# Linear attention and experts on one core: sums kept in PSUM, denominators on VectorE, one-piece half swap, another order on TensorE

## What is computed

```python
q = q * cos + _rotate_half(q) * sin
k = k * cos + _rotate_half(k) * sin
qf = jax.nn.elu(q) + 1.0
kf = jax.nn.elu(k) + 1.0
def step(carry, inp):
    state, z = carry
    q_s, k_s, v_s = inp
    state = state + k_s[..., :, None] * v_s[..., None, :]
    z = z + k_s
    num = jnp.einsum('bhe,bhed->bhd', q_s, state)
    den = jnp.einsum('bhe,bhe->bh', q_s, z)[..., None] + EPS
    return ((state, z), num / den)
```

## Time and profile before

| | us |
|---|---|
| median of 3 runs | 1166.92 (1160.2 to 1170.29) |
| the profiled execution | 1166.46 |
| its span, first to last instruction | 1164.7 |
| PE busy | 954.9 (82%) |
| DVE busy | 801.9 (69%) |
| ACT busy | 497.5 (43%) |
| POOL busy | 662.7 (57%) |

### The profile page before, as it was taken

The page is one execution under the profiler, slowest core; times in us unless marked ns, Lnnn a source line. Parts: engine busy times, 40 slices in busy tenths (PEclk is TensorE's granted clock), DMA queues, the critical chain, the costliest instruction groups (busy, mean ns, idle before and its releaser), DMA issues. The chain is left out here.

```text
span 1164.7 us, 14438 instructions
## 1 busy us (share of the span) xinstructions
PE 954.9 (82%) x4439; PEld 772.0 (66%) x4439; DVE 801.9 (69%) x1561; ACT 497.5 (43%) x818; POOL 662.7 (57%) x568
## 2 busy tenths in 40 slices
PE   5889999999999999898579999998319668687881
PEld 3677777877777787776368888887318556565661
DVE  7877777777777778787265888888736565655650
ACT  5444454544454544455241211120206555656550
POOL 2778777777877777787300333334352555556552
PEclk9899999999999999999789999998559899888995
DMA  7011111101111111117143334412154887877842
GB/s 259 6 45 47 47 40 41 50 32 41 50 37 50 42 42 41 42 37 239 68 154 139 127 137 139 144 71 111 52 204 142 246 250 227 239 227 210 265 77 37
DMA packets 51654, 129.65 MB, mean 111 GB/s; under 512 B 11144, under 2 KB 13704, under 8 KB 45424
## 3 DMA queue, kind: packets, MB, share of 16 engines
q1 hardware_dynamic: 40144, 114.52, 28.3%
q0 software_dynamic: 11424, 14.07, 7.1%
HBM read 105.53 MB, written 35.72 MB: 121 GB/s over the span
## 5 line engine op out<-in xcount | busy, mean ns | idle before, releaser
L585 POOL TENSOR_TENSOR a_t<-a_t 128x512 f32<-128x512 f32 x80 | 122.6, 1533 | 52.0 <-DVE a_t L361 52.0
L1076 DVE TENSOR_TENSOR w_l<-raw,w_h 128x1024 fp32r<-128x1024 f32 x96 | 114.3, 1221 | 52.4 <-ACT w_h L1069 46.9
L1169 POOL DMA_INDIRECT out<-m_y,si x38 | 69.2, 1822 | 115.4 <-issue 55.2
L616 POOL TENSOR_TENSOR a_A_l<-a_A,a_A_h 128x512 fp32r<-128x512 f32 x64 | 84.7, 1324 | 60.6 <-ACT a_A_h L474 60.6
L216 PE MATMUL a_PQ<-w_h,a_xT_h 128*128 128x512 f32 x384 | 113.8, 422 | 4.0 <-DVE w_l L347 3.3
L1069 ACT ACTIVATE w_h<-raw 128x1024 fp32r<-128x1024 f32 x96 | 97.8, 1061 | 39.5 <-PE m_PY L1233 39.4
L782 PE MATMUL r_PY<-w_h,r_o_h 128*128 128x512 f32 x256 | 102.9, 402 | 9.9 <-DVE r_o_l L864 9.9
L216 PE MATMUL a_PQ<-w_l,a_xT_h 128*128 128x512 f32 x384 | 104.7, 395 | 0.0
L216 PE MATMUL a_PQ<-w_h,a_xT_l 128*128 128x512 f32 x384 | 103.9, 393 | 0.0
L782 PE MATMUL r_PY<-w_l,r_o_h 128*128 128x512 f32 x256 | 101.9, 398 | 0.0
L782 PE MATMUL r_PY<-w_h,r_o_l 128*128 128x512 f32 x256 | 101.7, 397 | 0.0
(11 more groups left out here) (186 smaller groups left out, 2478.5 us busy)
## 6 DMA issues: line engine op xcount, KB each, us to landing
raw<-in_wgu SPq DMA_DIRECT2D x32, 1024.0 KB
oT<-a_o SPq DMA_DIRECT2D x64, 256.0 KB, 2.5
raw<-in_wd SPq DMA_DIRECT2D x32, 512.0 KB, 5.9
v_l<-oT SPq DMA_DIRECT2D x11, 1024.0 KB, 5.6
v_h<-oT SPq DMA_DIRECT2D x5, 1024.0 KB, 5.4
out<-r_x SPq DMA_DIRECT2D x18, 256.0 KB, 2.0
a_xin<-in_x SPq DMA_DIRECT2D x16, 256.0 KB, 3.2
v_l<-in_wq SPq DMA_DIRECT2D x4, 1024.0 KB, 13.5
```

Source lines behind the costliest of these rows:

```text
L585: eng.tensor_tensor(t1[:, r % 2, :], t1[:, r % 2, :], t2[:, r % 2, :], ALU.add).then_inc(sm["xr"], 1)
L616: eng.tensor_tensor(A_l[:, n % 2, :], A[:, n % 2, :], f(A_h[:, n % 2, :]), ALU.subtract).then_inc(sm["Al"], 1)
L1076: eng.tensor_tensor(low, src, high.bitcast(F32), ALU.subtract).then_inc(sm["m_wl"], 1)
L1169: eng.indirect_dma_start(out[:, :], bass.IndirectOffsetOnAxis(ap=si[:, i:i + 1], axis=0), y[:, e % 2, t, :], None, compute_op=ALU.add).the ...
```

## The change

- `turned` now also transposes x; the bank PX is given up. Key sums have a bank of their own, PZ, and the state one, PU. `sum_k` adds the lower part of the chunk's sums onto what the bank holds, and `rest_k`, after `z_copy`, adds the other part, so that each row then holds the sum over all tokens so far. `update` adds to PU from chunk to chunk; S, `state`, z_h and z_l are gone, and S_h and S_l are made from PU (S_l on VectorE).
- `times_z` is gone. `reduce` makes four `tensor_tensor_reduce` over 128 columns each, which multiply, sum and add 1e-6.
- `rotate` makes t2 with one instruction of 128x512 that reads the halves swapped.
- The projections of a chunk come in the order K, Q0, Q1, V, Q2, Q3. On TensorE `score` stands right behind the projections, then transposes, then `attend` and `update`. VectorE begins an iteration with `reduce` and `feature_q` of earlier groups. K_h, K_l and z have two buffers for one, QT_h and QT_l three for two, V_h and V_l two for three.
- Eight weight pieces are split ahead of the loop, and four in each of the first iterations. Wo is loaded an iteration later.

```diff
         def unit_v(c):
-            return 6 * c + 1
+            return 6 * c + 3
 
         def unit_q(n):
-            return 6 * (n // 4) + 2 + n % 4
+            return 6 * (n // 4) + (1, 2, 4, 5)[n % 4]
...
-                    if c >= 1:
-                        eng.wait_ge(sm["S"], c)
-                    eng.matmul(PM[:, :], tri_r[:, :], K_h[:, :], start=True, stop=False)
-                    last = eng.matmul(PM[:, :], tri_r[:, :], K_l[:, :], start=False, stop=c == 0)
-                    if c > 0:
-                        eng.matmul(PM[:, :], last_r[:, :], z_h[:, :], start=False, stop=False)
-                        last = eng.matmul(PM[:, :], last_r[:, :], z_l[:, :], start=False, stop=True)
-                    last.then_inc(sm["zc"], 1)
+                    eng.matmul(PZ[:, :], tri_r[:, :], K_h[:, c % 2, :], start=c == 0, stop=False, skip_group_check=True)
+                    eng.matmul(PZ[:, :], tri_r[:, :], K_l[:, c % 2, :], start=False, stop=True,
+                               skip_group_check=True).then_inc(sm["zc"], 1)
+
+                def rest_k(c):
+
+                    eng.wait_ge(sm["z"], c + 1)
+                    eng.matmul(PZ[:, :], rest_r[:, :], K_h[:, c % 2, :], start=False, stop=False, skip_group_check=True)
+                    eng.matmul(PZ[:, :], rest_r[:, :], K_l[:, c % 2, :], start=False, stop=True, skip_group_check=True)
 
...
                 def update(c):
-                    eng.wait_ge(sm["zl"], c + 1)
-                    eng.wait_ge(sm["z"], c + 1)
+
+                    eng.wait_ge(sm["pqfree"], unit_v(c) + 1)
+                    if c >= 1:
+                        eng.wait_ge(sm["Sl"], c)
                     for g in range(4):
                         cols = slice(g * P, (g + 1) * P)
                         steps = [(K_h, V_h), (K_h, V_l), (K_l, V_h)]
                         for s, (a, b) in enumerate(steps):
-                            last = eng.matmul(PM[:, cols], a[:, cols], b[:, c % 3, cols],
-                                              start=s == 0, stop=s == 2)
+                            last = eng.matmul(PU[:, cols], a[:, c % 2, cols], b[:, c % 2, cols],
+                                              start=c == 0 and g == 0 and s == 0, stop=s == 2, skip_group_check=True)
                     last.then_inc(sm["u"], 1)
 
                 turn_x(0)
                 for n in range(NG + 5):
                     c, g = divmod(n, 4)
                     if g == 0 and c < NC:
-                        project(unit_k(c), c, 0)
-                        project(unit_v(c), c, 1)
+                        project(unit_k(c))
+                    if g == 2 and c < NC:
+                        project(unit_v(c))
                     if n < NG:
-                        project(unit_q(n), c, 2 + g)
-                    if 0 <= n - 5 < NG:
-                        attend(n - 5)
-                    if g == 0 and 1 <= c < NC:
-                        update(c - 1)
+                        project(unit_q(n))
+                    if 0 <= n - 4 < NG:
+                        score(n - 4)
                     if g == 1 and c < NC:
                         eng.wait_ge(sm["f"], rot_k(c) + 1)
-                        turned(fK[:, :], turn_k(c))
+                        turned(fK[:, :], turns["k", c])
                         sum_k(c)
                     if 0 <= n - 3 < NG:
                         eng.wait_ge(sm["fs"], n - 2)
-                        turned(fQ[:, (n - 3) % 3, :], turn_q(n - 3))
+                        turned(fQ[:, (n - 3) % 3, :], turns["q", n - 3])
+                    if 0 <= n - 5 < NG:
+                        attend(n - 5)
+                    if g == 1 and 1 <= c < NC:
+                        update(c - 1)
                     if g == 2 and c + 1 < NC:
                         turn_x(c + 1)
-                    if 0 <= n - 4 < NG:
-                        score(n - 4)
+                    if g == 3 and c + 1 < NC:
+                        rest_k(c)
...
                     if r >= 2:
                         eng.wait_ge(sm["f"], r - 1)
                     q = heads(PQ[u % 2][:, :])
-                    a, b = heads(t1[:, r % 2, :]), heads(t2[:, r % 2, :])
-                    sn = tab[:, c % 2, 1, :]
-                    eng.tensor_tensor(a, q, spread(tab[:, c % 2, 0, :]), ALU.mult)
-                    eng.tensor_tensor(b[:, :, 0:64], q[:, :, 64:128], spread(sn[:, 0:64]), ALU.mult)
-                    eng.tensor_tensor(b[:, :, 64:128], q[:, :, 0:64], spread(sn[:, 64:128]), ALU.mult).then_inc(sm["pqfree"], 1)
+                    swapped = q.rearrange("p h (s d) -> p h s d", s=2)[:, :, ::-1, :]
+                    sn = tab[:, c % 2, 1, :].rearrange("p (s d) -> p s d", s=2).unsqueeze(1).broadcast_to([P, 4, 2, 64])
+                    eng.tensor_tensor(heads(t1[:, r % 2, :]), q, spread(tab[:, c % 2, 0, :]), ALU.mult)
+                    eng.tensor_tensor(heads(t2[:, r % 2, :]).rearrange("p h (s d) -> p h s d", s=2), swapped, sn,
...
-                    eng.wait_ge(sm["m"], n + 1)
+
+                    c, g = divmod(n, 4)
+                    if g == 0:
+                        eng.wait_ge(sm["z"], c + 1)
+                    eng.wait_ge(sm["f"], rot_q(n) + 1)
                     if n >= 2:
                         eng.wait_ge(sm["fs"], n - 1)
-                    d = den[:, n % 2, :]
-                    eng.tensor_reduce(d, heads(m[:, :]), axis=AX, op=ALU.add).then_inc(sm["den"], 1)
+                    for h in range(4):
+                        cols = slice(h * P, (h + 1) * P)
+                        last = eng.tensor_tensor_reduce(m[:, cols], fQ[:, n % 3, cols], z[:, c % 2, g * P:(g + 1) * P],
+                                                        1.0, 1e-6, ALU.mult, ALU.add, den[:, n % 2, h:h + 1])
+                    last.then_inc(sm["den"], 1)
                     eng.wait_ge(sm["den"], n + 1)
-                    eng.tensor_scalar_add(d, d, 1e-6).then_inc(sm["den1"], 1)
-                    eng.wait_ge(sm["den1"], n + 1)
-                    eng.reciprocal(d, d).then_inc(sm["rden"], 1)
+                    eng.reciprocal(den[:, n % 2, :], den[:, n % 2, :]).then_inc(sm["rden"], 1)
...
+                def s_low(c):
+                    eng.wait_ge(sm["Sh"], c + 1)
+                    eng.tensor_tensor(S_l[:, (c + 1) % 2, :], PU[:, :], f(S_h[:, (c + 1) % 2, :]),
+                                      ALU.subtract).then_inc(sm["Sl"], 1)
...
                 weight_low(0)
                 xT_low(0)
-                for i in range(1, 12):
-                    weight_low(i)
-                rotate(unit_k(0), rot_k(0), 0)
-                for i in range(12, 16):
-                    weight_low(i)
-                v_low(0)
-                for i in range(16, 24):
+                for i in range(1, 8):
                     weight_low(i)
                 for n in range(NG + 5):
                     c, g = divmod(n, 4)
-                    if g == 0 and 0 < c < NC:
+                    if 0 <= n - 2 < NG:
+                        reduce(n - 2)
+                    if 0 <= n - 1 < NG:
+                        feature_q(n - 1)
+                    if g == 2 and 1 <= c < NC:
+                        s_low(c - 1)
+                    if g == 0 and c < NC:
                         rotate(unit_k(c), rot_k(c), c)
-                        feature_q(n - 1)
+                    if c == 0:
+                        for k in range(4):
+                            weight_low(4 * (g + 2) + k)
+                    if g == 2 and c < NC:
                         v_low(c)
                     if n < NG:
                         rotate(unit_q(n), rot_q(n), c)
-                    if g == 0 and c < NC:
-                        feature_k(c)
-                    if g != 0 and n - 1 < NG or n == NG:
-                        feature_q(n - 1)
-                    if 0 <= n - 2 < NG:
-                        reduce(n - 2)
+                    if 0 <= n - 4 < NG:
+                        masked(n - 4)
                     if g == 1 and c < NC:
                         turn_low_k(c)
                     if 0 <= n - 3 < NG:
                         turn_low_q(n - 3)
-                    if 0 <= n - 4 < NG:
-                        masked(n - 4)
-                    if g == 1 and c < NC:
-                        z_low(c)
-                    if g == 0 and 1 <= c < NC:
-                        state(c - 1)
-                    if g == 0 and c + 1 < NC:
-                        stats(c + 1)
+                    if g == 0 and c < NC:
+                        feature_k(c)
+                    if n == 0:
+                        stats(1)
                     if g == 1 and c + 1 < NC:
                         normal(c + 1)
                     if g == 2 and c + 1 < NC:
                         xT_low(c + 1)
+                    if g == 3 and c + 2 < NC:
+                        stats(c + 2)
...
+                    if c == 0:
+                        for k in range(4):
```

(42 more changed lines are left out.)

174 lines of the change are left out of this document (71 added, 103 removed).

## The result

The changed kernel takes 1100.9 us (median of 4 runs, 1097.3 to 1106.4) against 1166.6 us (1160.2 to 1170.3): the ratio is 0.945, interval 0.939 to 0.951. 1101.0 was forecast. The profiled execution has a span of 1101.5 us. The total hides one large miss, in the start.

A forecast was written before the change was run, and what follows sets the result against it. TensorE was nearest the bound, needing 29.34 us of a 33.66 us chunk, the rest waits for A_l and what follows. Chunks -48.4, last chunk -1.7, tail -14.2, start -1.0: -65.3, from 1166.46 to 1101 us, range 1085 to 1135.

The forecast's parts named there:

- Order on TensorE: Score moved ahead of transposes and attend: the wait for A_l goes, worth at most 4.3 us a chunk.
- GpSimd: GpSimd loses four products and S_l per chunk, 26.2 to 19 us; its slack means this saves nothing by itself.
- The product with a sum: VectorE's product with sum over 128 columns: about 0.27 us, starts 0.20 apart, read 0.08; VectorE about 24 us a chunk.
- Collisions: VectorE's two-source products alternate with GpSimd: one 1.29 us instruction waited out in `reduce`, VectorE's iteration 5.9 us.
- Key chain: K_l, needed 8.9 us after its projection, takes about 9.5: 0.7 us of waiting a chunk (bounds 0 and 2.3).
- the prediction's second rival: Key chain late by more than 2 us in each chunk and the clock falls: 32.4 a chunk, 1135 us; chance 0.11.
- State and key sums in PSUM: Same number of matmuls on TensorE; S_l goes to VectorE in place of the sum, 0.7 each; no change.
- Start: Only 8 of 24 weight pieces split before the loop; Q2's and Q3's just as late: -1 us (bounds -3, +2).
- Tail: Stage after the last projection: 19.5 us for 33.7 (bounds 17 and 24), as scores no longer stand behind `attend`.
- both middle rivals: More collisions (1146 us, chance 0.12) and late key chain (1135 us, chance 0.11).
- The rival of more collisions: Two more GpSimd instructions get in per group of VectorE products: about 33.0 us a chunk, 1146 us; chance 0.12.
- The slower rival: GpSimd's sums, A_l and K_l all end up between VectorE's products: VectorE 37 us a chunk, 1208 us; chance 0.05.

The follow-up runs named there:

- e3: Changed kernel with TensorE's old order (attend and update before transposes, score last), masking behind the transpose's low part, output copy first on ScalarE: 1157.9 us, ratio 0.993.
- e6: Kernel before with only the new order (score, transposes, attend on TensorE, with the places of mask and output copy): 1121.7 us, ratio 0.961.
- e5: Changed kernel with one extra 128x512 multiplication, result unread, on GpSimd at the end of each iteration: 1145.9 us, ratio 0.985.
- e7: Kernel before with only the denominators changed: four products with sum on VectorE replace GpSimd's multiplication and VectorE's sum and addition: 1147.9 us, ratio 0.983.
- e12: Changed kernel with the key chain moved ahead and one extra multiplication per iteration on GpSimd: 1129.4 us, ratio 0.969.
- e8: Changed kernel with one extra 128x512 multiplication, result unread, on VectorE at the end of each iteration: 1123.5 us, ratio 0.965.
- e9: Changed kernel with the key chain moved ahead on VectorE, ScalarE and GpSimd, and one extra multiplication per iteration on VectorE: 1107.9 us, ratio 0.949.
- e11: Changed kernel with only the key chain (K's feature, K_h, K_l) moved ahead on VectorE, ScalarE and GpSimd: 1094.0 us, ratio 0.938.
- e1: Changed kernel with only weight splitting moved: all high parts ahead of ScalarE's loop, low parts 8 to 23 in the first iteration: 1094.0 us, ratio 0.937.

## Why the prediction came out right, step by step

That the total was right to within 1 us is luck: two errors met. The chunks, last chunk and tail gave more than forecast, and the start took it back. That it lies in the range is not luck, since either error alone would have left it within 12 us of the forecast. By the prediction's own terms: chunks -48.4 forecast, -53.3 with its border (-56.2 with the right one); last chunk -1.7, measured -2.5; tail -14.2, measured -15.3; start -1.0, measured +10.0 by its border (+12.8 by the right one). The untouched rest, taken as 0, gave -2.0.

1. Order on TensorE: the mechanism was right. No wait for A_l is left, and e3 brings it back; the granted clock of the chunks rose from 0.96 to 1.00, in e6 too. Of the 56.2 us of the chunks 22.7 are TensorE's busy time (435.55 to 412.85) and 33.5 its idle time. The size was too large for the order by itself: it is worth 2.4 us a chunk (e6). The sum gave it nearly all of the gain, 4.3 less the key chain and small gaps; the whole change brought 4.0.
2. GpSimd: the size was right, 273.54 / 14 = 19.5 us a chunk for 19. The sentence that its slack makes this worth nothing by itself failed: e5 loses 2.7 us a chunk by putting 5 us back, as GpSimd's instructions then lengthen VectorE's list. e7 gains 1.05 with this part and the products together, with VectorE's own list 27 us longer over the fourteen chunks.
3. The product with a sum: 0.28 us (277 ns at the least) for 0.27, starts 0.21 apart for 0.20, the read of the accumulator 0.08 as taken. The Trainium skill's half rate for two SBUF sources that are not bf16 (Vector Engine (DVE) Microarchitecture Reference, Points that are easy to get wrong) would have been seen in the feature, which still takes 0.68 us, and in the product, 0.28 us and not the 0.4 that the prediction gave for it; it is not. But VectorE came to 25.5 us a chunk, not 24.
4. Collisions were mis-sized in both directions. A group of products has 4 x 0.454 = 1.8 us instead of 4 x 0.28 = 1.1: 0.7 us lost a group, where 1.29 was taken. x's normalization, uncounted, now collides too (1.21 us for 0.53), with one tensor source where the prediction saw the matter in instructions with two. The Trainium skill (GPSIMD Engine Reference, Specifications) has the two engines contend for SBUF where VectorE has two inputs there or runs in a 2-port mode; e5 and e12 agree, with the 44 us that 66 us of GpSimd cost VectorE.
5. Key chain: the right chain, and the size too large. Forecast 0.7 us of waiting a chunk; in the steady chunks there is none, with 0.4 us of slack, and only three of the fourteen wait for K_l, so a steady chunk is 29.55 us: the floor of 29.34 and 0.2 of gaps. The prediction's working does not come out either: 6 + 0.7 + 0.6 + 1.3 + 2 x 1.29 is 11.2 and not 9.5, and would have given its upper bound of 2.3. In the chunk shown K's projection ends at 268.53 and K_l at 277.12, 8.6 us later: the feature started after 5.3 us and not 6, and K_l waited 0.45 us for A_l where two whole instructions were taken. e5, e8, e9 and e11 show that it is the first chain to be late, the one that the prediction's second rival named; that rival itself, more than 2 us of waiting a chunk, did not come.
6. State and key sums in PSUM: TensorE's need of 29.34 us held, the steady chunk leaves at most 0.2 us for an extra cost. It was not tried alone, nor was the half swap in one piece.
7. Start: the step that failed, in sign, and five times its upper bound of +2. It put the pieces of Q2 and Q3 "just as late as now", by where they stand in the lists. What it left out is what stands ahead of them there: features and products that wait for an earlier projection. Q3's projection began at 50.18 us, in the kernel before at 38.40. e1 shows it by undoing that alone, for 10.6 of the 12.8 us.
8. Tail: 18.4 us for 19.5, at clock 1.00. Of the 17.8 us between last K projection and last attend, the order alone gives 11 (e6).

In the chances the forecast and both middle rivals but for 0.03 add up to 0.92, not 0.93.

The rival of more collisions (1146) did not come, but e5 lands on its number, 1145.9: it needs 5 us more of GpSimd a chunk. The slower rival was far: even that run stays 1.5% below the kernel before.

## What to carry to other kernels

- Work that is needed once at the start and is interleaved into a loop's lists must be checked item by item for what stands ahead of it: if that waits for the consumer of the item before, the start becomes a chain of round trips. Here it cost 10.6 us of start (e1), and mending it together with the key chain won 14.5 in all.
- An engine can be idle a quarter of the time (GpSimd in e5) and still cost, if its instructions hold up another engine's. Price such a load by what it adds to the other's list; here two thirds of it (e5, e12).
- When the bound engine is fully busy, measure how much room the others have (an instruction more in each iteration, whose result nobody reads): it names the chain that is late next, which can then be moved ahead. Here that gave 0.35 us a chunk in the changed kernel and 1.0 in the one with more load (e11, e9).

## What the runs showed of the hardware

- GpSimd's 128x512 instruction goes between two of a row of back-to-back VectorE instructions, each with two SBUF sources, and the one behind it lasts about the rest of it longer: 1.38 and 1.37 us for 0.28 in one group. GpSimd's own instruction is stretched as well, 1.74 us for 1.3 (274.08, begun 0.23 us after K's feature). It is not only instructions with two tensor sources: x's normalization has one and took 1.21 us for 0.53.
- After idle times of 3.7 and 3.1 us in the start TensorE's groups of four take up to 2.05 us instead of 1.07: its 1.2 GHz level instead of 2.4 (granted clock 0.56 and 0.64 over these two projections, 1.00 in the chunks).
- A product with its sum over 128 columns costs 0.21 us from start to start on VectorE, and the read of its accumulator, 0.08 us, lies fully under the next one.
